# Fused attention and expert feed-forward block on Trainium2: a new tile order in the last group of heads and a rewritten last finish

## Chip, cores and metric

One core of a Trainium2 chip. The metric is the device time of one execution in microseconds; lower is better. A profile is one execution of its own, taken by the hardware profiler; its span runs from the first to the last instruction.

## The reference

A pre-norm transformer block on x of shape (1, 2048, 128) in float32: causal attention with 16 heads of 8 dimensions and rotary embedding, then a feed-forward part with a base layer, a shared low-rank expert and six low-rank experts of which the two with the largest gates count.

```python
def attn(x, w_qkv, w_out):                       # 16 heads, dh = 8
    q, k, v = split(x @ w_qkv)                   # to heads; rope on q and k
    scores = where(causal, q @ k.T * dh ** -0.5, finfo.min)
    return (softmax(scores) @ v).merge_heads() @ w_out

def ffn(x, base_W, base_b, shared_A, shared_B, routed_A, routed_B, router_W, router_b):
    base_out = x @ base_W.T + base_b
    shared_out = (x @ shared_A.T) @ shared_B.T                # rank 16
    logits = x @ router_W.T + router_b                        # 6 experts
    gate = softmax(logits)
    sparse_w = two largest gates of a row, others 0
    sparse_w = sparse_w / (sum(sparse_w) + 1e-6)
    routed = sum over e of sparse_w[e] * ((x @ routed_A[e].T) @ routed_B[e].T)
    return base_out + shared_out + routed

x = x + attn(layernorm(x), ...)
x = x + ffn(layernorm(x), ...)                   # layernorm without scale and shift, eps 1e-5
```

## The kernel before

The 2048 rows are 16 tiles of 128. `PREPS` are the stretches for which keys, queries and values are prepared, `PIECES` the query stretches that attention runs over, `FINISHES` those for which the output projection and the feed-forward part are done. The last piece and the last finish are tiles 14 and 15. Heads are worked in `NG` = 4 groups of four.

For one piece and group, `group_work` (line 85) lists the units: a unit is the scores of one key tile for the piece's query rows. In a piece of two query tiles a unit of kind "wide" is 128 keys by 256 query rows by four heads (1024 columns in PSUM), and the last key tile is a unit "half" with 128 query rows (512 columns). Only the last two units, key tiles t0 and t0 + 1, lie on the diagonal and are masked. Two units make a block; `plan` (line 94) numbers units and blocks, and `values` are issued a block at a time.

All engines walk the same list in their own program order, tied by semaphores:

- TensorE: `scores(u)` (line 926) into one of `NS` = 3 PSUM buffers, then `values(b)` (line 945) for blocks that are due, `LAG` = 5 units after their last unit, then `job(n)` (line 992) for other products.
- ScalarE: the exponential of unit u (line 588), straight from PSUM into one of `NPB` = 8 SBUF buffers `pbuf`; it signals `exp_ready`.
- GpSimd: masks (line 537) on diagonal units only, after their exponential; it signals `masked`. `values` of a block with a diagonal unit waits for `masked`.
- VectorE: `evacuate` (line 638) when a group's last block is done: transposes the sums in `po` and, in the last finish, divides them by the row sums (`normalise`, line 629). `take(n)` (line 731) does VectorE's part of the other jobs.
- SyncE: loads and stores.

A finish is the job list `FINISH` = A, O, M1, M2, M3, X, R, W1, W2, U, F. A: VectorE transposes the attention output into `feat`. O: output projection, added to the residual `xs` (line 779). M1, M2, M3: row moments (lines 614, 617), inverse root (lines 385, 386, 374 to 380), normalised rows `ln` (line 394). X: TensorE transposes `ln` (line 1018), VectorE copies it to `feat` (line 787). R: down projection with `wdown` (line 1021), whose 118 columns are 16 shared, 96 routed and 6 router columns; VectorE adds the router bias, subtracts the row maximum (lines 791 to 794) and copies the 112 low-rank columns to `low_rank` (line 796); ScalarE takes the exponential (line 599). W1 and W2: VectorE ranks the six gates by comparing each with each (lines 714 to 719) and scales the low-rank columns by the kept shares (lines 724 to 729, 803). U: TensorE transposes `low_rank` (line 1029), VectorE copies it to `lowT` (line 806). F: up projection onto the base products (lines 972, 1034), added to `xs` (line 809), which `store` (line 476) writes out. The constant 1 in column `RD` of `low_rank` brings in the bias of the base layer.

The earlier finishes are spread among the units (`PLACES`). The last one, `TAIL_JOBS`, runs alone after the loop. Each job of VectorE that feeds TensorE ends with a wait on its own last instruction (`then`) and a marker instruction (line 812) that signals `job_fed`. In the tail TensorE issues, before its product of each job, a number of matmuls that only keep it at work (`keep_warm`, line 1079):

```python
WARM = {"O": 8, "X": 16, "R": 3, "U": 16, "F": 3}
```

Of the kernel before, what the change touches and what calls it, by code (L numbers as in the profile page):

```python
# [80 lines left out]
FINISH_OF = [next(f for f, (t0, n) in enumerate(FINISHES) if t0 <= at < t0 + n) for at, _ in PIECES]  # L81
SWAPPED_PREPS = 3


def group_work(t0, tiles):

    if tiles == 4:
        return ([[("full", kt, (0,)), ("full", kt, (1,))] for kt in range(t0 + 1)]
                + [[("ends", t0 + 1, (0,)), ("ends", t0 + 1, (1,))], [("mid", t0 + 2, (0, 1))]])
    wide = [("wide", kt, (0, 1)) for kt in range(t0 + 1)] + [("half", t0 + 1, (0, 1))]  # L90
    return [wide[n:n + 2] for n in range(0, len(wide), 2)]


def plan():


    units, blocks = [], []
    for i, (t0, tiles) in enumerate(PIECES):
        for g in range(NG):
            work = group_work(t0, tiles)  # L100
            for n, members in enumerate(work):
                mine = list(range(len(units), len(units) + len(members)))
                for kind, kt, pairs in members:
                    units.append(dict(i=i, g=g, kind=kind, kt=kt, pairs=pairs, diagonal=kt >= t0, block=len(blocks)))
                blocks.append(dict(i=i, g=g, units=mine, first=n == 0, last=n == len(work) - 1,
                                   diagonal=any(units[u]["diagonal"] for u in mine)))
    return units, blocks
# [54 lines left out]
WARM = {"O": 8, "X": 16, "R": 3, "U": 16, "F": 3}  # L162
# [23 lines left out]
def schedule():  # L186


    jobs, at = [], {}
    for i, (mine, places) in enumerate(zip(ORDER, PLACES)):  # L190
        assert len(mine) == len(places)
        for job, place in zip(mine, places):
            at.setdefault(FIRST_UNIT[i] + place, []).append(len(jobs))
            jobs.append(job)
    tail = list(range(len(jobs), len(jobs) + len(FINISH)))
    jobs += [(name, NFINISH - 1) for name in FINISH]
    return jobs, at, tail


JOBS, JOBS_AT, TAIL_JOBS = schedule()  # L200
# [9 lines left out]
def build(nc, x, w_qkv, rope_c, rope_s, w_out, w_down, w_up, w_base, router_b, ident, head_sum,  # L210
# [3 lines left out]
    with ExitStack() as ctx:  # L214
# [59 lines left out]
        rank = sb("rank", [P, TC, E])  # L274

# [9 lines left out]

        def bank(n):

            return ps[:, 1, 0, :] if n == TAIL_JOBS[-1] else pm[:, :]
# [42 lines left out]
        y_ready = sem("y_ready")  # L331
        stored = sem("stored")
# [114 lines left out]
        def _(sp):  # L447
# [53 lines left out]
            for f in range(1, NFINISH):  # L501
                store(f)
            sp.wait_ge(stored, 16 * NFINISH)
# [38 lines left out]
        def _(act):  # L542
# [54 lines left out]
            nt = FINISHES[-1][1]  # L597
            act.wait_ge(logits_ready, NFINISH)
            nc.scalar.activation(gate[:, 0:nt, :], lg[:, 0:nt, :], ACT.Exp).then_inc(logits_exp, 1)  # L599

        @block.vector
        def _(dve):
# [128 lines left out]
            def take(n):  # L731
# [4 lines left out]
                product = bank(n)  # L736
# [74 lines left out]
                if n in FEEDS:  # L811
                    nc.vector.engine_nop().then_inc(job_fed, 1)  # L812

# [107 lines left out]
            for n in TAIL_JOBS:  # L921
                take(n)

        @block.tensor
        def _(pe):
# [66 lines left out]
            def job(n):  # L992
# [5 lines left out]
                product = bank(n)  # L998
# [20 lines left out]
                elif name == "R":  # L1019
# [3 lines left out]
                    if n in TAIL_JOBS:  # L1023
                        ins.then_inc(job_full, 1)
                        base(bank(TAIL_JOBS[-1]), nt)
                        return
# [3 lines left out]
                elif name == "F":  # L1030
                    if n not in TAIL_JOBS:
                        base(product, nt)
# [50 lines left out]

            pe.wait_ge(warm_ready, 1)
# [39 lines left out]
            for n in TAIL_JOBS:  # L1124
                keep_warm(WARM.get(JOBS[n][0], 0), kst[:, 0, 0:P], kst[:, 0, 0:CH])
                job(n)
# [56 lines left out]
```

## Time and profile before

| | us |
|---|---|
| median of 3 runs (lowest to highest) | 319.71 (319.04 to 320.12) |
| profiled execution, device time | 319.8 |
| its span | 318.1 |
| TensorE busy (matmuls) in the span | 285.8 (90%) |
| ScalarE | 269.6 (85%) |
| VectorE | 146.3 (46%) |
| GpSimd | 57.5 (18%) |
| mean granted TensorE clock | 0.973 of full |

The page gives each engine's busy time, and the same in 40 equal slices. The timeline shows instructions in order of time, merged where several of a line follow each other ("x4"); a bracket behind one says how long its engine had been idle and what released it. PEld is TensorE's weight load, which overlaps its matmuls, and DVE is VectorE, ACT ScalarE, POOL GpSimd, SP SyncE. A float32 product shows as two instructions. A merged row runs from the start of its first instruction to the end of its last. Ends of matmuls are modelled.

### The profile page before, as it was taken

What the parts mean: (1) busy time and instruction counts of PE and PEld (TensorE: products, weight loads), DVE (VectorE), ACT (ScalarE), POOL (GpSimd) and SP (SyncE); (2) the same over time, 40 slices, a digit from 0 to 9 for tenths busy, and PEclk for the clock granted to TensorE, in tenths of its full rate; (3) what the DMA queues carried; (4) which work ended last, traced back from release to release, by engine and by line L of the source; (5) the groups of instructions that cost most, each with busy time, mean ns of one, the idle gap of its engine ahead of it and who ended that gap; (6) DMA issues with size and microseconds to landing.
All of it is one profiled execution on the core that took longest, in us unless ns stands there. A gap on an engine that the chain in (4) does not pass through costs nothing.

```text
span 318.1 us, 7501 instructions
## 1 busy us (share of the span) xinstructions
PE 285.8 (90%) x3006; PEld 103.8 (33%) x3008; DVE 146.3 (46%) x425; ACT 269.6 (85%) x300; POOL 57.5 (18%) x129
## 2 busy tenths in 40 slices
PE   7948883989899989899999998999999999999896
PEld 2613241222223422123313313443533333433353
DVE  6775596468875376956241003651000514101064
ACT  8567584779999798999999999999999999999700
POOL 0485141031330300403003020101001010110100
PEclk9966998799999999999999999999999999999999
DMA  6333137000550000160000100000100000000000
GB/s 173 112 93 92 26 103 190 10 1 2 152 148 0 23 15 1 35 165 2 0 3 0 36 2 2 0 3 2 35 2 3 2 2 0 2 19 2 3 0 16
DMA packets 15400, 11.75 MB, mean 37 GB/s; under 512 B 2033, under 2 KB 14178, under 8 KB 15362
## 3 DMA queue, kind: packets, MB, share of 16 engines
q1 hardware_dynamic: 14866, 10.90, 12.6%
q8 instruction: 25, 0.41, 0.6%
q10 hardware_dynamic: 432, 0.20, 0.2%
q0 software_dynamic: 64, 0.13, 0.1%
q14 instruction: 13, 0.11, 0.1%
HBM read 3.88 MB, written 1.05 MB: 16 GB/s over the span
## 4 chain that ended last, share of the span: by engine, by line
PE 37%; ACT 22%; DVE 21%; issue 15%; DMA 2%; SPq 1%; DVEq 1%; POOL 0%; ACTq 0%; POOLq 0%
ACT pbuf L588 22%; PE po L962 17%; PE ps L940 9%; PE pm L978 3%; DVE rest L665 3%; DMA xs<-x_dram 2%; PE ps L1082 2%; DVE rot L672 2%; DVE absmax L696 1%; PE pm L1021 1%; PE pm L1015 1%; DVE oq L647 1%; DVE rot L659 1%; DVE rest L682 1%; PE pm L972 1%
## 5 line engine op out<-in xcount | busy, mean ns | idle before, releaser
L588 ACT ACTIVATE pbuf<-ps 128x1024 f32<-128x1024 f32 (+1 forms) x280 | 253.9, 1068 | 24.6 <-PE ps L940 24.2
L962 PE MATMUL po<-pbuf,va 128*9 128x256 f32 (+3 forms) x1792 | 146.7, 433 | 9.3 <-DVE oq L647 7.0
L940 PE MATMUL ps<-qst,kst 64*128 64x256 bf16 (+3 forms) x896 | 97.7, 303 | 8.1 <-ACT pbuf L588 3.4
L537 POOL TENSOR_SCALAR_AFFINE_SELECT pbuf<-pbuf 128x256 f32<-128x256 f32 (+1 forms) x104 | 48.9, 492 | 231.6 <-ACT pbuf L588 230.4
L940 PEld LDWEIGHTS ps<-qst,kst 64*128 64x128 bf16 x896 | 30.3, 95 | 104.0 <-ACT pbuf L588 77.2
L962 PEld LDWEIGHTS po<-pbuf,va 128*9 128x9 f32 x1792 | 35.6, 90 | 66.7 <-issue 42.8
L647 DVE STREAM_TRANSPOSE oq<-po 128x256 f32<-128x256 f32 (+1 forms) x24 | 12.9, 536 | 84.7 <-PE po L962 84.4
L665 DVE TENSOR_TENSOR rest<-pm,sinT 32x512 f32<-32x512 f32 x16 | 11.0, 687 | 0.3
L978 PE MATMUL pm<-xnT,wqkv 128*128 128x512 f32 x16 | 9.0, 644 | 1.9 <-DVEq L812 1.3
L1082 PE MATMUL ps<-kst 128*128 128x512 bf16 x44 | 10.5, 379 | 0.2 <-issue 0.2
L806 DVE COPY lowT<-pm 113x512 f32<-113x512 f32 (+1 forms) x5 | 2.9, 585 | 16.6 <-PE pm L1029 16.6
L614 DVE BATCH_NORM_STATS2 stats<-xs 128x6 f32<-128x128 f32 x32 | 7.1, 282 | 4.8 <-DMA xs<-x_dram 3.3
L599 ACT ACTIVATE gate<-lg 128x12 f32<-128x12 f32 x1 | 0.2, 213 | 10.4 <-DVE lg L794 10.4
L809 DVE TENSOR_TENSOR xs<-pm,xs 128x512 f32<-128x512 f32 (+1 forms) x4 | 2.5, 624 | 12.0 <-PE pm L1034 12.0
L779 DVE TENSOR_TENSOR xs<-pm,xs 128x512 f32<-128x512 f32 (+1 forms) x5 | 2.9, 585 | 9.2 <-PE pm L1015 9.2
L1082 PE MATMUL ps<-xnT 128*128 128x512 bf16 x16 | 5.2, 499 | 1.5 <-DVE xnT L868 1.5
L672 DVE TENSOR_TENSOR rot<-rot,rest 128x512 f32<-128x512 f32 (+1 forms) x10 | 6.1, 608 | 0.3
L1082 PEld LDWEIGHTS ps<-kst 128*128 128x128 bf16 x46 | 4.4, 97 | 4.5 <-issue 0.2
L545 ACT COPY kst<-fillers 128x2048 f32<-128x2048 f32 x3 | 5.7, 1897 | 0.0
L549 ACT COPY qst<-fillers 128x2048 f32<-128x2048 f32 x3 | 5.7, 1895 | 0.0
L682 DVE TENSOR_TENSOR rest<-rot,parts 128x512 f32<-128x512 f32 (+1 forms) x8 | 5.6, 694 | 0.3
L787 DVE COPY feat<-pm 128x512 f32<-128x512 f32 (+1 forms) x5 | 2.9, 585 | 5.6 <-PE pm L1018 5.6
(115 smaller groups left out, 184.6 us busy)
## 6 DMA issues: line engine op xcount, KB each, us to landing
qst<-parts SPq DMA_DIRECT2D x18, 128.0 KB, 2.4
kst<-parts SPq DMA_DIRECT2D x18, 128.0 KB, 2.5
xs<-x_dram SPq DMA_DIRECT2D x4, 256.0 KB, 4.1
cosT<-rope_c_dram SPq DMA_DIRECT2D x4, 256.0 KB, 4.4
sinT<-rope_s_dram SPq DMA_DIRECT2D x4, 256.0 KB, 5.6
out_dram<-xs SPq DMA_DIRECT2D x3, 256.0 KB, 2.3
kst<-parts SPq DMA_DIRECT2D x11, 64.0 KB, 2.1
qst<-parts SPq DMA_DIRECT2D x8, 64.0 KB, 2.0
```

What stands on the lines that cost most here:

```text
L537: ins = nc.gpsimd.affine_select(out=edge, in_=edge, compare_op=ALU.is_ge, fill=0.0, base=0, pattern=[[0, edge.shape[1]], [1, P]], channel_ ...
L545: nc.scalar.copy(kst[:, :, c * CH:(c + 1) * CH].bitcast(F32), fillers[:, 0:1].unsqueeze(2).broadcast_to([P, NP, CH // 2])).then_inc(filled, 1)
L588: nc.scalar.activation(probs[:, :, 0:width], ps[:, u % NS, :, 0:width], ACT.Exp, scale=SCALE).then_inc(exp_ready, 1)
L614: ins = nc.vector.bn_stats(stats[:, t, :], xs[:, tile + t, :])
L647: nc.vector.transpose(oq[:, g, mine, :].rearrange("p b r -> p (b r)"), po[:, 0:nt * P]).then_inc(o_free, 1)
L665: ins = nc.vector.tensor_tensor(rest[there:there + HALF, which, cols], product[here:here + HALF, :], sinT[here:here + HALF, c % 2, cols], ...
L672: return nc.vector.tensor_tensor(rot[:, which, cols], rot[:, which, cols], rest[:, which, cols], ALU.add)
L682: then(nc.vector.tensor_tensor(rest[:, which, cols], rot[:, which, cols], parts[:, which, 0, cols], ALU.subtract))
L940: ins = nc.tensor.matmul(ps[:, u % NS, e, place:place + n], side(kst, e)[:, g * 2 + pair, key:key + P], side(qst, e)[:, g * 2 + pair, q:q ...
L962: ins = nc.tensor.matmul(po[32 * j:32 * j + DH + 1, q0:q0 + n], va[:, kt, g * GH + j, :], pbuf[:, u % NPB, at:at + n], start=blk["first"] ...
L978: return nc.tensor.matmul(product, wqkv[:, which, :], xnT[:, chunk(p) % 2, local(p)], start=True, stop=True)
L1082: nc.tensor.matmul(ps[:, 1, 1, :], left, right, start=True, stop=True)
```

## The change

In the last group of heads of the last piece, the unit list is turned so that the two masked units come first, and the last block is split into two blocks of one unit. The tail jobs are replaced by one written-out sequence `end_of_chunk` on VectorE and TensorE, with semaphores of its own and no marker instructions:

- rows are only centred (mean subtracted) before they are transposed; the inverse root is computed after that. The scale of a row is applied to the logits, and to the final sum in the last instructions; the bias column gets the reciprocal of the scale (variance + eps, times the inverse root).
- ScalarE makes the copy of the transposed rows, and that of the 16 shared columns; the 96 routed columns are read by VectorE from PSUM as they are gated.
- experts are ranked by their logits, not by their exponentials. The comparison "greater" goes to a buffer of its own, `end_over`, and the difference to the maximum to `above`.
- the final sum is made tile by tile, and each tile has a store of its own.
- warm-up matmuls: 8, 7, 2, 14, 2 in place of 8, 16, 3, 16, 3.

```diff
+END, END_TILES = FINISHES[-1]
...
-def group_work(t0, tiles):
+def group_work(t0, tiles, last):
...
     wide = [("wide", kt, (0, 1)) for kt in range(t0 + 1)] + [("half", t0 + 1, (0, 1))]
+    if last:
+        wide = wide[-2:] + wide[:-2]
     return [wide[n:n + 2] for n in range(0, len(wide), 2)]
...
     for i, (t0, tiles) in enumerate(PIECES):
         for g in range(NG):
-            work = group_work(t0, tiles)
+            end = (i, g) == (NPIECE - 1, NG - 1)
+            work = group_work(t0, tiles, end)
+            if end:
+                work[-1:] = [[unit] for unit in work[-1]]
             for n, members in enumerate(work):
...
-WARM = {"O": 8, "X": 16, "R": 3, "U": 16, "F": 3}
+WARM_O, WARM_X, WARM_R, WARM_U, WARM_F = 8, 7, 2, 14, 2
...
-    tail = list(range(len(jobs), len(jobs) + len(FINISH)))
-    jobs += [(name, NFINISH - 1) for name in FINISH]
-    return jobs, at, tail
-JOBS, JOBS_AT, TAIL_JOBS = schedule()
...
-            for f in range(1, NFINISH):
+            for f in range(1, NFINISH - 1):
                 store(f)
-            sp.wait_ge(stored, 16 * NFINISH)
+            for t in range(END_TILES):
+                sp.wait_ge(y_ready, NFINISH + t)
+                sp.dma_start(out_t[:, END + t:END + t + 1, :], xs[:, END + t:END + t + 1, :]).then_inc(stored, 16)
+            sp.wait_ge(stored, 16 * (NFINISH - 1 + END_TILES))
...
-            nt = FINISHES[-1][1]
-            act.wait_ge(logits_ready, NFINISH)
-            nc.scalar.activation(gate[:, 0:nt, :], lg[:, 0:nt, :], ACT.Exp).then_inc(logits_exp, 1)
+            act.wait_ge(end_rows_turned, 1)
+            nc.scalar.copy(feat[:, 0:END_TILES * P], pm[:, 0:END_TILES * P]).then_inc(end_input, 1)
+            act.wait_ge(end_logits, 1)
+            nc.scalar.activation(gate[:, 0:END_TILES, :], above[:, 0:END_TILES, 0, :], ACT.Exp).then_inc(end_exp, 1)
+            by_tile = pm[:, 0:END_TILES * P].rearrange("p (t d) -> p t d", t=END_TILES)
+            nc.scalar.copy(low_rank[:, 0:END_TILES, 0:R], by_tile[:, :, 0:R]).then_inc(end_shared, 1)
...
+            def end_of_chunk():
+                f, nt = NFINISH - 1, END_TILES
+                tiles, wide = slice(END, END + nt), nt * P
+                by_tile = pm[:, 0:wide].rearrange("p (t d) -> p t d", t=nt)
+                last = ps[:, 1, 0, 0:wide].rearrange("p (t d) -> p t d", t=nt)
+                scale = rstd[:, 0, :]
+                nc.vector.transpose(feat[:, 0:wide],
+                                    att[:, f % 2, 0:wide // SQ, :, :].rearrange("p b g d -> p (b g d)")).then_inc(end_turned, 1)
+                dve.wait_ge(end_summed, 1)
+                then(nc.vector.tensor_tensor(xs[:, tiles, :], by_tile, xs[:, tiles, :], ALU.add))
+                spread(END, 0, nt)
+                for t in range(nt):
+                    nc.vector.tensor_scalar(ln[:, t, :], xs[:, END + t, :], mv[:, 0, t, 0:1], None,
+                                            ALU.subtract).then_inc(end_rows, 1)
+                inverse_sqrt(nc.vector, then, 0, nt)
+                then(nc.vector.tensor_tensor(low_rank[:, 0:nt, RD], var[:, 0, 0:nt], scale[:, 0:nt], ALU.mult))
+                dve.wait_ge(ffn_in, 16 * 5)
+                dve.wait_ge(end_down, 1)
+                mine, top, less = lg[:, 0:nt, :], chosen[:, 0:nt], above[:, 0:nt, 0, :]
+                for t in range(nt):
+                    ins = nc.vector.scalar_tensor_tensor(lg[:, t, :], by_tile[:, t, RD:RD + E], scale[:, t:t + 1],
+                                                         rbias[:, :], ALU.mult, ALU.add)
+                then(ins)
+                then(nc.vector.tensor_reduce(top, mine, AX.X, ALU.max))
+                nc.vector.tensor_tensor(less, mine, top.unsqueeze(2).broadcast_to([P, nt, E]),
+                                        ALU.subtract).then_inc(end_logits, 1)
+                shape = [P, nt, E, E]
+                this, other = mine.unsqueeze(3).broadcast_to(shape), mine.unsqueeze(2).broadcast_to(shape)
+                tied, over = ties[:, 0:nt], end_over[:, 0:nt]
+                then(nc.vector.tensor_tensor(tied, other, this, ALU.is_equal))
+                nc.vector.tensor_tensor(over, other, this, ALU.is_gt)
+                then(nc.vector.tensor_tensor(tied, tied, low[:, :, :].unsqueeze(1).broadcast_to(shape), ALU.mult))
+                then(nc.vector.tensor_tensor(over, over, tied, ALU.add))
+                then(nc.vector.tensor_reduce(rank[:, 0:nt, :], over, AX.X, ALU.add))
+                dve.wait_ge(end_exp, 1)
+                kept, total, share = rank[:, 0:nt, :], small[:, 0:nt], gate[:, 0:nt, :]
+                nc.vector.tensor_reduce(total, share, AX.X, ALU.add)
+                then(nc.vector.scalar_tensor_tensor(kept, kept, 1.5, share, ALU.is_lt, ALU.mult))
+                then(nc.vector.tensor_reduce(top, kept, AX.X, ALU.add))
+                then(nc.vector.scalar_tensor_tensor(total, total, 1e-6, top, ALU.mult, ALU.add))
+                then(nc.vector.reciprocal(total, total))
+                then(nc.vector.tensor_tensor(share, kept, total.unsqueeze(2).broadcast_to([P, nt, E]), ALU.mult))
+                dve.wait_ge(end_shared, 1)
+                nc.vector.tensor_tensor(low_rank[:, 0:nt, R:RD].rearrange("p t (e r) -> p t e r", e=E),
+                                        by_tile[:, :, R:RD].rearrange("p t (e r) -> p t e r", e=E),
+                                        gate[:, 0:nt, :].unsqueeze(3).broadcast_to([P, nt, E, R]),
+                                        ALU.mult).then_inc(end_routed, 1)
+                dve.wait_ge(end_low_turned, 1)
+                nc.vector.tensor_copy(lowT[0:RD + 1, 0:nt, :].rearrange("p t d -> p (t d)"),
+                                      pm[0:RD + 1, 0:wide]).then_inc(end_low, 1)
+                dve.wait_ge(end_full, 1)
+                for t in range(nt):
+                    nc.vector.scalar_tensor_tensor(xs[:, END + t, :], last[:, t, :], scale[:, t:t + 1], xs[:, END + t, :],
+                                                   ALU.mult, ALU.add).then_inc(y_ready, 1)
...
+            def end_of_chunk():
+                hot = kst[:, 0, 0:P], kst[:, 0, 0:CH]
+                tile = lambda t: slice(t * P, (t + 1) * P)
+                keep_warm(WARM_O, *hot)
+                pe.wait_ge(end_turned, 1)
+                for t in range(END_TILES):
+                    ins = nc.tensor.matmul(pm[:, tile(t)], feat[:, tile(t)], wout[:, :], start=True, stop=True)
+                ins.then_inc(end_summed, 1)
+                keep_warm(WARM_X, *hot)
+                for t in range(END_TILES):
+                    pe.wait_ge(end_rows, t + 1)
+                    ins = nc.tensor.transpose(pm[:, tile(t)], ln[:, t, :], idf[:, :])
+                ins.then_inc(end_rows_turned, 1)
+                keep_warm(WARM_R, *hot)
+                pe.wait_ge(end_input, 1)
+                for t in range(END_TILES):
+                    ins = nc.tensor.matmul(pm[:, t * P:t * P + RD + E], feat[:, tile(t)], wdown[:, :], start=True, stop=True)
+                ins.then_inc(end_down, 1)
+                base(ps[:, 1, 0, :], END_TILES)
+                keep_warm(WARM_U, *hot)
+                pe.wait_ge(end_shared, 1)
+                pe.wait_ge(end_routed, 1)
+                for t in range(END_TILES):
+                    ins = nc.tensor.transpose(pm[0:RD + 1, tile(t)], low_rank[:, t, 0:RD + 1], idf[:, :])
+                ins.then_inc(end_low_turned, 1)
+                keep_warm(WARM_F, *hot)
+                pe.wait_ge(end_low, 1)
+                for t in range(END_TILES):
+                    ins = nc.tensor.matmul(ps[:, 1, 0, tile(t)], lowT[0:RD + 1, t, :], wup[:, :], start=False, stop=True,
+                                           skip_group_check=True)
+                ins.then_inc(end_full, 1)
...
-            for n in TAIL_JOBS:
-                keep_warm(WARM.get(JOBS[n][0], 0), kst[:, 0, 0:P], kst[:, 0, 0:CH])
-                job(n)
+            end_of_chunk()
 
 
 def rope_tables(order):
```

## Rows read from the trace of the kernel before

**Rows 1.** Page, span and granted TensorE clock in 40 slices (tenths).

```profile
span 318.1 us, 7501 instructions
...
PEclk9966998799999999999999999999999999999999
```

**Rows 2.** Windows: stretch, its length, busy us per engine, granted clock, DMA share, GB/s.

```profile
53.00:56.00 3.00, 0.90 (x12) 0.42 (x16) 1.95 (x2) 0.00 (x0) 0.00 (x0) 0.50 0.80 223
284.00:300.00 16.00, 14.85 (x228) 5.43 (x228) 0.88 (x3) 16.00 (x19) 1.73 (x4) 1.00 0.01 3
```

**Rows 3.** Timeline, loop's end: start, us, engine, line, operation, count, idle before.

```profile
297.18 1.05 PE L962 MATMUL po<-pbuf,va 128*9 128x256 f32 x16
...
298.16 0.29 PE L940 MATMUL ps<-qst,kst 64*128 64x128 bf16 x4
...
298.38 1.91 PE L962 MATMUL po<-pbuf,va 128*9 128x256 f32 x32
299.62 1.35 POOL L537 TENSOR_SCALAR_AFFINE_SELECT pbuf<-pbuf 128x512 f32<-128x512 f32 x3 [12.89 <-ACT pbuf L588]
...
301.03 0.84 PE L962 MATMUL po<-pbuf,va 128*9 128x256 f32 x16 [0.73 <-POOL pbuf L537]
```

**Rows 4.** Line 588's last three exponentials: ns min/median/max, first and last start.

```profile
L588 ACT ACTIVATE pbuf<-ps x3: 853/1255/1269, 297.4 to 299.2; 128x1024 f32<-128x1024 f32 x2, 128x512 f32<-128x512 f32 x1
```

**Rows 5.** Timeline, first half of the last finish.

```profile
303.54 0.52 PEld L1015 LDWEIGHTS pm<-wout,feat 128*128 128x128 f32 x4 [0.34 <-DVEq L812]
...
305.55 0.17 DVE L385 TENSOR_SCALAR var<-mv 128x2 f32<-128x2 f32 x1
...
307.33 0.60 DVE L394 TENSOR_SCALAR ln<-xs,mv,rstd 128x128 f32<-128x128 f32 x2
...
308.05 0.44 PE L1018 MATMUL pm<-idf,ln 128*128 128x128 f32 x2 [0.34 <-DVEq L812]
...
309.06 0.70 PE L1021 MATMUL pm<-wdown,feat 128*128 128x118 f32 x4
```

**Rows 6.** Groups by line and shape, ScalarE: busy us, mean ns, idle before.

```profile
L545 ACT ACT_TABLE_LOAD x1 | 1.3, 1283 | 0.8 <-PEq L1177 0.8
...
L554 ACT COPY xnT<-pm 128x256 f32<-128x256 f32 x1 | 0.4, 373 | 0.2 <-PE pm L1090 0.2
```

**Rows 7.** Timeline, second half of the last finish, to the transposes.

```profile
309.80 0.17 DVE L791 TENSOR_TENSOR lg<-pm,rbias 128x12 f32<-128x12 f32 x1 [0.85 <-PE pm L1021]
309.94 3.23 PEld L1082 LDWEIGHTS ps<-kst 128*128 128x128 bf16 x16
...
310.20 0.17 DVE L794 TENSOR_TENSOR lg<-lg,small 128x12 f32<-128x12 f32 x1
310.29 0.38 DVE L796 COPY low_rank<-pm 128x224 f32<-128x224 f32 x1
...
310.72 0.23 DVE L714 TENSOR_TENSOR ties<-gate 128x72 f32<-128x72 f32 x1
...
313.13 0.36 DVE L803 TENSOR_TENSOR low_rank<-low_rank,gate 128x192 f32<-128x192 f32 x1
...
313.60 0.47 PE L1029 MATMUL pm<-idf,low_rank 128*113 128x128 f32 x2
```

**Rows 8.** Timeline, last sum and store.

```profile
315.39 0.42 DVE L809 TENSOR_TENSOR xs<-ps,xs 128x256 f32<-128x256 f32 x1 [0.86 <-PE ps L1034]
315.85 0.37 SPq L479 DMA_DIRECT2D out_dram<-xs  x1
```

**Rows 9.** DMA issues of the stores: count, KB each, us to landing.

```profile
out_dram<-xs SPq DMA_DIRECT2D x3, 256.0 KB, 2.3
...
out_dram<-xs SPq DMA_DIRECT2D x2, 128.0 KB, 1.8
```

**Rows 10.** Timeline of SyncE's queue: two issues in a row.

```profile
30.19 0.34 SPq L491 DMA_DIRECT2D wout<-w_out_dram  x1
30.58 0.43 SPq L491 DMA_DIRECT2D wdown<-w_down_dram  x1
```

More of the change, by code:

```diff
@@ L194, in schedule @@
             jobs.append(job)
-    tail = list(range(len(jobs), len(jobs) + len(FINISH)))
-    jobs += [(name, NFINISH - 1) for name in FINISH]
-    return jobs, at, tail
-JOBS, JOBS_AT, TAIL_JOBS = schedule()
+    return jobs, at
+JOBS, JOBS_AT = schedule()
 IS_PRODUCT = [name in PRODUCT_JOBS for name, _ in JOBS]
@@ L274, in build @@
         rank = sb("rank", [P, TC, E])
+        end_over = sb("end_over", [P, END_TILES, E, E])
         rmax = sb("rmax", [P, TC, H])
@@ L284, in build @@
         pm = ctx.enter_context(nc.psum_tensor("pm", [P, CH], F32))
-        def bank(n):
-            return ps[:, 1, 0, :] if n == TAIL_JOBS[-1] else pm[:, :]
         def first_bank(p, name):
@@ L331, in build @@
         y_ready = sem("y_ready")
+        end_turned = sem("end_turned")
+        end_summed = sem("end_summed")
+        end_rows = sem("end_rows")
+        end_rows_turned = sem("end_rows_turned")
+        end_input = sem("end_input")
+        end_down = sem("end_down")
+        end_logits = sem("end_logits")
+        end_exp = sem("end_exp")
+        end_shared = sem("end_shared")
+        end_routed = sem("end_routed")
+        end_low_turned = sem("end_low_turned")
+        end_low = sem("end_low")
+        end_full = sem("end_full")
         stored = sem("stored")
@@ L735, in take @@
                     dve.wait_ge(job_full, PRODUCTS[n])
-                product = bank(n)
+                product = pm[:, :]
                 if name in FINISH:
@@ L920, in _ @@
                         evacuate(b)
-            for n in TAIL_JOBS:
-                take(n)
+            end_of_chunk()
         @block.tensor
@@ L997, in job @@
                 pe.wait_ge(job_fed, FED[n])
-                product = bank(n)
+                product = pm[:, :]
                 tile = lambda t: slice(t * P, (t + 1) * P)
@@ L1022, in job @@
                                                start=True, stop=True)
[L1023 to L1026, printed above, removed]
                 elif name == "U":
@@ L1030, in job @@
                 elif name == "F":
-                    if n not in TAIL_JOBS:
-                        base(product, nt)
+                    base(product, nt)
                     for t in range(nt):
@@ L1123, in _ @@
                     values(b)
-            for n in TAIL_JOBS:
-                keep_warm(WARM.get(JOBS[n][0], 0), kst[:, 0, 0:P], kst[:, 0, 0:CH])
-                job(n)
+            end_of_chunk()
 def rope_tables(order):
```

## The prediction

> **What bounds the kernel now.** I read the page first: the span is 318.1 us and TensorE's granted clock is at its upper level (2.4 GHz) from the eleventh of the 40 slices to the end [rows 1]. The profiled run took 319.8 us, so 1.7 us lie around the span; the median of the three runs is 319.71, 0.1 below it. All sums below are made against the 319.8 run and then lowered by 0.1.
>
> Next the table of windows. From 284 to 300 us ScalarE is busy 16.00 of 16.00 us while TensorE has 14.85 [rows 2]: the loop over score tiles is bound by ScalarE's exponentials until the last one. Then the timeline of the loop's end. What the reader should see [rows 3]: the scores of the last unit at 298.16, then two whole blocks of value matmuls (32 matmuls, to 300.29), then GpSimd's masks of the last two tiles from 299.62 to about 301.0 (1.35 us busy in three instructions), and only then, at 301.03, the last 16 value matmuls, over at 301.87. The exponentials themselves [rows 4]: three start between 297.4 and 299.2, so 0.91 apart; the last full one starts at 298.3 and takes 1.269 us, so it ends at about 299.56 (it overlaps its neighbours in the record); the last one, half as wide, takes 0.853 and ends at 300.05. So a half tile holds ScalarE for 0.5 us and a full one for 0.91. The masks start 0.06 us after the 299.56 end: that is my price for a bare handoff between engines. Masks, not exponentials, release the last block: 0.98 us after the last exponential.
>
> After that one serial chain runs to the end, and VectorE carries most of it [rows 5, 7, 8]. TensorE fills its gaps with warm-up matmuls in program order, so two lines have to be compared in every gap.
>
> **Part 1: the masked tiles first, in the last group only.** The group has 15 full tiles and one half tile either way; ScalarE's work is the same and ends at about 300.06. The value matmuls after it no longer wait for masks, and the last block has one tile, not two. But TensorE takes its work in order. In the new order every exponential from the second on ends 0.91 - 0.50 = 0.41 earlier than the one in the same position now, except the last. TensorE follows ScalarE there, so its block of 297.18 and the scores at 298.16 [rows 3] move to about 296.77 and 297.75. The last scores are those of a full tile, some 0.1 us longer than the 0.22 until 298.38, so the remaining blocks start at 298.07. They are 16 + 16 + 8 + 8 matmuls. Two blocks in a row take 1.91 us, one alone at full width 1.05, so a block adds 0.86: 298.07 + 3 x 0.86 + 0.19 = 300.84. The last exponential is done at 300.06, in time for the last 8 matmuls at about 300.22. New end 300.84 against 301.87: gain 1.03. Best case, bound by ScalarE alone: 300.06 + 0.06 + 0.43 + 0.19 = 300.74, gain 1.13. Worst case: the two half tiles, now one unit apart, let ScalarE run dry. Between two releases of a score buffer lie two exponentials, 0.91 + 0.50 = 1.41 us, for a block of values (0.86) and a scores unit (up to 0.4), so there is just room; the same combination now passes once between groups without idle ScalarE [rows 2]. I allow 0 to 0.25 us of loss and take nothing.
> The masks of the new first block stand in GpSimd's queue behind the three instructions of the group before. Their values are due after the seventh scores of the group, some 4 us after their exponentials, and 2 x 1.35 us of masks [rows 3] fit in that: nothing. That cover would be gone if GpSimd had other work; it has none there.
>
> **Part 2: from the attention output to the logits.** VectorE's transposes, reciprocal and product right after the last block stay. The output projection is released by a VectorE marker instruction now (0.34 idle until 303.54 [rows 5]); the marker goes, which could give 0.05, but the eight warm-ups in front of it stay and end at about the same time: I take 0 of 0 to 0.05.
> Then the order changes. Now: moments done at 305.52, nine small instructions of the inverse root from 305.55 to 307.33 (1.78), two row normalisations of 0.60, marker, transposes at 308.05, VectorE's copy, down projection at 309.06, logits at 309.80 [rows 5, 7]. From 305.55 that is 4.25 us.
> New, from the same point A: two centrings, 0.60 (the same two rows of 128 elements, one operation less on each). They release the transposes; VectorE goes on with the nine instructions (1.78) and one more small one (0.20), so it is ready for the logits at A + 0.60 + 0.02 + 1.78 + 0.20 + 0.02 = A + 2.62. The other line: transposes start at A + 0.66, take 0.3 to 0.44, ScalarE's copy of 128x256 takes 0.37 [rows 6], its handoffs 0.06 to 0.12 each, the down projection 0.74 from 309.06 to 309.80: A + 2.2 to 2.4. VectorE is last, and the projection is hidden behind the inverse root. Gain 4.25 - 2.62 = 1.63. If ScalarE's or TensorE's handoffs are slower than in the rows, up to 0.3 of it goes. The two copies put on ScalarE stand behind an idle queue after 300.06. The trace has one table load in all, at the start, and copies and exponentials alternate later without another [rows 6]: no switching cost.
>
> **Part 3: routing.** Now, from the logits to the transposes: 309.80 to 313.60, 3.80 us [rows 7]. A small waited instruction costs 0.20 (1.78 / 9), one that nothing waits for 0.09 (310.20 to 310.29), the 72-element ones 0.23 and about 0.26 waited. New: two logit instructions in place of one, 0.28; maximum 0.20; difference 0.09; comparison "equal" 0.26; "greater", now unwaited, 0.15; product, sum, count 0.26 + 0.27 + 0.26; total, unwaited, 0.09; kept, sum, combination, reciprocal, share 5 x 0.20; gating 0.36; handoff 0.06, and 0.05 for the added waits: 3.33. The large removed term is the copy of 128x224 out of PSUM, which stood on VectorE from 310.29 until the comparison at 310.72: 0.43, now ScalarE's (at most the 0.37 of [rows 6], from an exponential that no longer holds the comparisons up). Gain 0.47, between 0.3 and 0.55. TensorE's line there: down projection done by A + 2.4, base products, then 14 warm-ups at 3.23 / 15 = 0.215 [rows 7], 3.0 us, the first at most 0.14 after the logits' release: that ends at A + 5.5, while VectorE ends at A + 5.9. It stays covered; with 16 it would be about even.
>
> **Part 4: after the gating.** The copy of the turned low-rank features loses its marker: gain 0.05. At the end one sum of 0.42 and one store [rows 8] become two scaled sums of 128 columns and two stores. By the pair in [rows 5], 0.60 for both and, an estimate, 0.34 for the first. The first store is issued at +0.38; the second can follow 0.39 later (30.19 to 30.58, [rows 10]), at +0.77, against +0.46 now, so 0.31 later. It moves half the bytes. The stores of 256 KB land after 2.3 us, that of 128 KB after 1.8 [rows 9], so 64 KB less should give back 0.25; that leaves -0.06. If landing stays at 1.8, it is -0.31. I take -0.10, range -0.4 to 0. The Trainium skill (DMA: Bandwidth & Descriptors, Anatomy of one DMA) speaks against this part: a DMA's fixed cost of some 2 us doesn't depend on size, and bytes add only bytes / 436 GB/s. By that, halving 128 KB gives back an estimated 0.15 us, and this part would be -0.16. The fixed part agrees in kind with the trace's 1.8 us for a small store.
>
> **Sum.** 1.03 + 0 + 1.63 + 0.47 + 0.05 - 0.10 = 3.08 us. 319.8 - 3.08 - 0.1 = 316.6 us. Sum of the worst ends: 0.78 + 1.33 + 0.30 - 0.40 = 2.0, so 317.7; of the best: 1.13 + 0.05 + 1.63 + 0.55 + 0.05 = 3.4, so 316.3.
>
> **Rivals.** (a) TensorE's line takes VectorE's place in the finish: warm-ups, base products and handoffs are late in both long gaps by 0.3 to 0.4 each. For it: the margins are only 0.2 and 0.4 us. Against it: both are computed from rows at the same clock. Time 317.3.
> (b) Part 1 gives only 0.2: ScalarE runs dry near the two half tiles, or the three value blocks, in program order, are still what ends last. For it: 48 value matmuls stand behind the last scores in both versions, and TensorE has 1.15 us of slack in 16. Against it: the 0.73 us that TensorE idled for the masks is really gone. Time 317.4.
> (c) Slower: TensorE's clock falls to 1.2 GHz in the finish, since there are 33 warm-ups there instead of 46. The trace shows the lower level between 53 and 56 us (granted 0.50 [rows 2]), where TensorE was at work for 0.90 of 3 us. At it a warm-up takes 0.43 (twice 0.215): the 8, 7 and 14 would then outlast VectorE by about 1.7 + 1.1 + 2.9, and the matmul groups would add some 2: 7.7 us, time 324.3. It decides once the clock falls before about 307. Against it: the longest idle stretch of TensorE after the change is shorter than the 0.73 us before 301.03, which leaves the clock at its upper level now. The Trainium skill (TensorE: Matmul & The Clock Gate, What's actually happening) says the gate follows how busy the engine has been recently; by it the denser end would keep the clock.
> (d) (a) and (b) together, with a late second store: 318.0 to 318.9, too near to be told from no change when over 318.75.
>
> **Chances.** About 0.3% (0.96 us) is what a measurement of this kernel can tell from no change. Forecast, 316.6 within 0.6: 0.60. (a) 0.16, (b) 0.10, (d) 0.06, more gain than the best sum (below 316.0): 0.05, (c) 0.03. Faster 0.92, same 0.05, slower 0.03. The range takes in the forecast, (a) and (b): 315.9 to 317.9.
>
> **What would show it.** Right: the last value block over at 300.8 with no idle TensorE before it; logits 2.6 us after the moments with VectorE, not TensorE, released last; 3.3 us from logits to the transposes; last store issued 0.8 us after the last product. Wrong: gaps in ScalarE between 285 and 290, a clock below 1.0 after 300, VectorE idle before the logits or before the gating, a table load, or a second store that lands over 2 us after its issue.

## The result and the profile after

| | before | after |
|---|---|---|
| median, us (lowest to highest) | 319.71 (318.76 to 320.30) | 316.36 (315.97 to 316.77) |
| ratio, 95% interval | | 0.990 (0.9876 to 0.9925) |
| profiled execution, us | 319.8 | 316.77 |
| its span, us | 318.1 | 315.0 |

The changed kernel is 3.35 us faster by the medians and 3.0 by the profiled runs. The page after the change, to be read beside [rows 1]: span, and granted TensorE clock in tenths for each of 40 slices.

```profile
span 315.0 us, 7475 instructions
...
PEclk9976998699999999999999999999999999999999
```

The clock is at its upper level to the end, as before.

Executions differ in when they come to the end of the loop: what lies ahead of it is the same code, but the first mark below stands at 283.49 to 284.50 in the fourteen profiled executions. So I compare distances between marks that every version has, not clock times. The first mark is the start of the half tile's scores in the group before the last (283.92 before, 284.14 after); the others follow in the table. The one for the moments is the start of the second moment instruction (aggregation). The page rounds spans to a tenth; I use the trace's hundredths: 318.06 before, 315.03 after.

Where several profiled executions have the same code in a stretch, these distances agree within 0.02 us; so a difference of 0.1 us between two of them is read below as one of the code.

| stretch, us | before | after | gain | predicted |
|---|---|---|---|---|
| half tile's scores to the end of the last value block | 17.95 | 16.92 | 1.03 | 1.03 |
| to the moments (aggregation starts) | 3.40 | 3.34 | 0.06 | 0 |
| to the logits | 4.53 | 2.65 | 1.88 | 1.63 |
| to the second transposes | 3.80 | 3.47 | 0.33 | 0.47 |
| to the last product | 1.05 | 0.96 | 0.09 | 0.05 |
| to the end of the span | 3.41 | 3.55 | -0.14 | -0.10 |
| sum | 34.14 | 30.89 | 3.25 | 3.08 |

The rows behind it. Timeline of the changed kernel at the loop's end (start, us, engine, line, operation, count, idle before), to be read beside [rows 3]:

```profile
285.60 2.76 POOL L554 TENSOR_SCALAR_AFFINE_SELECT pbuf<-pbuf 128x512 f32<-128x512 f32 x6 [12.93 <-ACT pbuf L605]
...
296.97 1.05 PE L1037 MATMUL po<-pbuf,va 128*9 128x256 f32 x16
...
297.95 0.39 PE L1015 MATMUL ps<-qst,kst 64*128 64x256 bf16 x4
...
298.28 2.78 PE L1037 MATMUL po<-pbuf,va 128*9 128x256 f32 x48
300.31 0.24 PEld L1037 LDWEIGHTS po<-pbuf,va 128*9 128x9 f32 x8 [0.19 <-ACT pbuf L605]
```

The six masks from 285.60 are the three of the group before, which stood there already, and the three of the last group, which have moved here; TensorE waits for none of them. The last scores start at 297.95, and from 298.28 one unbroken run of 48 value matmuls ends at 301.06; where 0.73 us of idle TensorE stood in [rows 3] there is none. The only wait in it is the weight load of the last block for the last exponential, 0.19 us, which hides under the matmuls still running. ScalarE doesn't run dry near the two half tiles. Window of the changed kernel, to be read beside [rows 2]:

```profile
284.00:300.00 16.00, 14.78 (x232) 5.63 (x232) 0.88 (x3) 16.00 (x19) 2.70 (x6) 1.00 0.01 3
```

Timeline of the changed kernel from the output projection to the logits, beside [rows 5]:

```profile
302.67 0.52 PEld L1161 LDWEIGHTS pm<-wout,feat 128*128 128x128 f32 x4 [0.28 <-DVE feat L841]
...
304.69 0.48 DVE L847 TENSOR_SCALAR ln<-xs,mv 128x128 f32<-128x128 f32 x2
...
305.03 0.52 PE L1166 MATMUL pm<-idf,ln 128*128 128x128 f32 x2
305.08 0.16 DVE L399 TENSOR_SCALAR var<-mv 128x2 f32<-128x2 f32 x1
...
305.59 0.37 ACT L615 COPY feat<-pm 128x256 f32<-128x256 f32 x1 [5.33 <-PE pm L1166]
...
306.02 0.70 PE L1171 MATMUL pm<-wdown,feat 128*128 128x118 f32 x4
...
306.86 0.16 DVE L850 TENSOR_TENSOR low_rank<-var,rstd 128x2 f32<-128x2 f32 x1
...
307.05 0.35 DVE L855 SCALAR_TENSOR_TENSOR lg<-pm,rstd,rbias 128x6 f32<-128x6 f32 x2
307.44 0.17 DVE L858 TENSOR_REDUCE chosen<-lg 128x2 f32<-128x12 f32 x1
```

The order has turned round: rows are centred from 304.69, transposed from 305.03, ScalarE's copy runs from 305.59 to 305.96 and the down projection from 306.02 to 306.72; beside them, on VectorE, the inverse root runs from 305.08. VectorE is done at 307.02 and takes the logits at 307.05 with no wait. Note that the root starts 0.39 after the first centring, and that the two logit instructions take 0.39 until the maximum at 307.44.

Timeline of the changed kernel in the routing part, beside [rows 7]:

```profile
307.85 0.21 ACT L617 ACTIVATE gate<-above 128x12 f32<-128x12 f32 x1 [1.89 <-DVE above L859]
307.97 0.17 ACT L619 COPY low_rank<-pm 128x32 f32<-128x32 f32 x1
308.00 0.23 DVE L865 TENSOR_TENSOR end_over<-lg 128x72 f32<-128x72 f32 x1
...
310.01 0.36 DVE L878 TENSOR_TENSOR low_rank<-pm,gate 128x192 f32<-128x192 f32 x1
...
310.52 0.45 PE L1178 MATMUL pm<-idf,low_rank 128*113 128x128 f32 x2 [0.32 <-DVE low_rank L878]
```

ScalarE's exponential and its copy of the shared columns are over at 308.14, while VectorE compares. They are not waited for. The gating ends at 310.37 and the transposes start 0.15 later, after 0.32 us in which TensorE had no work left: VectorE is last here too.

Timeline of the last sums and stores, and then the issues of stores with KB each and us to landing, beside [rows 8, 9]:

```profile
312.23 0.61 DVE L887 SCALAR_TENSOR_TENSOR xs<-ps,rstd,xs 128x128 f32<-128x128 f32 x2 [0.81 <-PE ps L1183]
312.61 0.82 SPq L519 DMA_DIRECT2D out_dram<-xs  x2
```

```profile
out_dram<-xs SPq DMA_DIRECT2D x3, 256.0 KB, 2.3
...
out_dram<-xs SPq DMA_DIRECT2D x1, 128.0 KB, 1.9
out_dram<-xs SPq DMA_DIRECT2D x2, 64.0 KB, 1.6
```

### The profile page after: what moved, and what is told of

Same layout as the page of the kernel before. It is cut to its first block, busy times and chain, and to the rows that moved or that the text cites. A ratio compares the mean times of both kernels' runs of the same rounds, so it can differ in the third digit from the quotient of the medians.

```text
span 315.0 us, 7475 instructions
## 1 busy us (share of the span) xinstructions
PE 284.0 (90%) x2995; PEld 103.0 (33%) x2995; DVE 146.0 (46%) x426; ACT 270.1 (86%) x302; POOL 57.5 (18%) x129
## 3 DMA queue, kind: packets, MB, share of 16 engines
HBM read 3.88 MB, written 1.05 MB: 16 GB/s over the span
## 4 chain that ended last, share of the span: by engine, by line
PE 39%; DVE 23%; ACT 20%; issue 14%; DMA 2%; DVEq 1%; SPq 1%; ACTq 0%
ACT pbuf L605 19%; PE po L1037 19%; PE ps L1015 10%; PE pm L1053 3%; DVE rest L685 3%; DMA xs<-x_dram 2%; DVE rot L692 2%; DVE absmax L716 1%; DVE oq L667 1%; DVE rot L679 1%; DVE rest L702 1%; PE pm L1090 1%; PE pm L1096 1%; PE pm L1047 1%; DVE parts L709 1%
## 5 line engine op out<-in xcount | busy, mean ns | idle before, releaser
L1152 PE MATMUL ps<-kst 128*128 128x512 bf16 x33 | 8.0, 379 | 0.0
L679 DVE TENSOR_TENSOR rot<-pm,cosT 128x512 f32<-128x512 f32 x4 | 2.8, 692 | 5.6 <-PE pm L1053 5.1
L711 DVE TENSOR_TENSOR parts<-rest,parts 128x512 bf16<-128x512 f32 (+1 forms) x8 | 5.2, 645 | 0.3
L716 DVE TENSOR_REDUCE absmax<-rot 128x2 f32<-128x1024 f32 (+1 forms) x5 | 5.0, 996 | 0.0
```

What stands on the lines that cost most here:

```text
L716: then(nc.vector.tensor_reduce(absmax[:, :], rot[:, :, local(p)], AX.X, ALU.max, apply_absolute_value=True))
L1152: nc.tensor.matmul(ps[:, 1, 1, :], left, right, start=True, stop=True)
```

## Experiments

All have the computation of the reference except where it is said. The two parts alone and the better version at the end were timed several times; the others rest on one profiled execution each, and are read by the distances between marks, not by their total time. Clock times of these rows are those of their own execution.

**The two parts, each alone.** First the kernel before with the new order and the split only:

```diff
+    if last:
+        wide = wide[-2:] + wide[:-2]
...
+            if end:
+                work[-1:] = [[unit] for unit in work[-1]]
```

> Part 1 alone on the kernel before: masked units first in the last group, last block in two. Measured from the scores of the half tile of the group before to the end of the last value block: before 17.95 us. Theory (the wait for the masks was the cost, TensorE's program order is what is left): 16.92, no idle TensorE before the last block, total 1.0 us under before (318.7). Rival (b) (ScalarE runs dry at the two half tiles or the queue of value blocks ends at the same time anyway): 17.75, total 319.5.

Measured: 318.69 us median against 319.81, ratio 0.9968 (0.9948 to 0.9988). Timeline of this kernel, first and last mark of the loop's end:

```profile
283.69 0.29 PE L945 MATMUL ps<-qst,kst 64*128 64x128 bf16 x4
...
297.82 2.78 PE L967 MATMUL po<-pbuf,va 128*9 128x256 f32 x48
```

297.82 + 2.78 - 283.69 = 16.91 us, against 17.95. The wait for the masks is gone, and 48 matmuls in program order are what is left. Rival (b), with a gain of only 0.2 us, falls.

Then the changed kernel without these lines, so the new finish behind the old order:

> The new finish alone, with the old order of units and blocks. Theory (the two parts don't overlap): the loop ends as before (17.95), and the finish is 2.2 to 2.3 us shorter, total 317.4. Rival (a part of the finish's gain came from TensorE's line being earlier after part 1): under 1.8 us.

Measured: 317.65 us median, ratio 0.9929 (0.9904 to 0.9954); loop's end 17.94. Timeline, last value block of this kernel:

```profile
301.07 0.84 PE L1033 MATMUL po<-pbuf,va 128*9 128x256 f32 x16 [0.73 <-POOL pbuf L550]
```

The wait for the mask is back as it was. From the moments to the logits 2.65, to the second transposes 3.47, to the last product 0.96: the same as with both parts. Gains by the medians: 1.1 + 2.2 us, against 3.35 for both. The parts add up.

**The split of the last block.** The changed kernel without its second edit to the blocks:

```diff
-            if end:
-                work[-1:] = [[unit] for unit in work[-1]]
```

> The changed kernel with the last block of two units as one block. Theory: its 16 matmuls wait for the last exponential and then take 1.05 instead of 0.75, so the loop's end is 0.30 later than after the change (17.2 instead of 16.9 by the measure above). Rival (program order alone decides, the split is for nothing): no later.

Timeline of this kernel, the two marks:

```profile
284.42 0.28 PE L1013 MATMUL ps<-qst,kst 64*128 64x128 bf16 x4
...
298.55 3.09 PE L1035 MATMUL po<-pbuf,va 128*9 128x256 f32 x48
```

298.55 + 3.09 - 284.42 = 17.22 us against 16.92: the split is worth 0.30 of the 1.03 and the order alone 0.73. Whole block or not, the number of matmuls is the same; but the whole one holds the first tile's matmuls back until the last exponential.

**Warm-ups.** The changed kernel with the old numbers:

```diff
-WARM_O, WARM_X, WARM_R, WARM_U, WARM_F = 8, 7, 2, 14, 2
+WARM_O, WARM_X, WARM_R, WARM_U, WARM_F = 8, 16, 3, 16, 3
```

> The changed kernel with the old numbers of warm-ups (8, 16, 3, 16, 3). Theory (two lines in every gap; VectorE's is last by only 0.2 to 0.3 us now): the transposes of the centred rows start 1.5 later, the logits 1.35 later, and the gap before the second transposes gives 0.15 more, 1.5 us in all. Rival (VectorE's chain sets the end and warm-ups are free): under 0.2.

Timeline of this kernel: warm-ups, transposes, logits.

```profile
303.47 3.62 PE L1152 MATMUL ps<-kst 128*128 128x512 bf16 x16
...
306.92 0.38 PE L1166 MATMUL pm<-idf,ln 128*128 128x128 f32 x2
...
308.62 0.35 DVE L855 SCALAR_TENSOR_TENSOR lg<-pm,rstd,rbias 128x6 f32<-128x6 f32 x2 [1.35 <-PE pm L1171]
```

The sixteen warm-ups hold the transposes until 306.92, though the rows were ready at about 305.3, and the logits now wait 1.35 us for TensorE. From the moments to the logits 3.97 instead of 2.65 (+1.32), to the second transposes 3.59 instead of 3.47 (+0.12). Together that is 1.44, near the 1.5 expected; 0.06 comes back before the last product, so the old numbers would have taken 1.38 of the gain of 3.25. The rival, under 0.2, falls.

The changed kernel with none:

```diff
-WARM_O, WARM_X, WARM_R, WARM_U, WARM_F = 8, 7, 2, 14, 2
+WARM_O, WARM_X, WARM_R, WARM_U, WARM_F = 0, 0, 0, 0, 0
```

> The changed kernel with no warm-up in the finish. Theory (the clock falls when TensorE has little to do): the granted clock goes to 0.5 within the finish, the later matmul groups get longer, and the total is 0.5 to 1.5 us more. Rival (the finish is too short for a fall, VectorE sets the end): clock stays 1.0, total the same or up to 0.1 less.

Windows of this kernel (stretch, length, busy us of TensorE, weight load, VectorE, ScalarE, GpSimd, then granted clock, DMA share, GB/s), and then its matmul groups:

```profile
300.00:303.00 3.00, 1.38 (x20) 0.74 (x12) 1.32 (x4) 0.03 (x1) 0.00 (x0) 1.00 0.00 0
303.00:306.00 3.00, 0.90 (x5) 0.40 (x3) 2.53 (x13) 0.37 (x1) 0.00 (x0) 0.84 0.00 0
306.00:308.00 2.00, 1.99 (x8) 1.69 (x8) 1.31 (x9) 0.00 (x0) 0.00 (x0) 0.50 0.00 0
```

```profile
302.44 0.71 PE L1161 MATMUL pm<-wout,feat 128*128 128x128 f32 x4 [1.62 <-DVE feat L841]
...
304.79 0.65 PE L1166 MATMUL pm<-idf,ln 128*128 128x128 f32 x2 [1.64 <-DVE ln L847]
...
305.91 1.21 PE L1171 MATMUL pm<-wdown,feat 128*128 128x118 f32 x4 [0.46 <-ACT feat L615]
...
311.99 1.22 PE L1183 MATMUL ps<-wup,lowT 113*128 113x128 f32 x4 [0.52 <-DVE lowT L883]
```

TensorE was idle for 1.62 us before 302.44 and for 1.64 before 304.79; the granted clock, 1.00 up to 305, was 0.50 from 305.5 to the end (finer windows of the same execution). The down projection takes 1.21 us instead of 0.70, the last product 1.22 instead of 0.71. From the first mark to the end it is 32.13 us instead of 30.89: 1.24 more, although no warm-up is in anybody's way: 0.45 of it before the logits, 0.30 between the second transposes and the last product, 0.50 behind the start of that product. The two runs together: a warm-up costs nothing only while it ends ahead of the other line, and leaving all out costs 1.2. Numbers between 0 and 33 were not tried.

**What the copy on ScalarE is worth.** The changed kernel with that copy on VectorE, behind the centring:

```diff
-            nc.scalar.copy(feat[:, 0:END_TILES * P], pm[:, 0:END_TILES * P]).then_inc(end_input, 1)
...
+                dve.wait_ge(end_rows_turned, 1)
+                nc.vector.tensor_copy(feat[:, 0:wide], pm[:, 0:wide]).then_inc(end_input, 1)
                 inverse_sqrt(nc.vector, then, 0, nt)
```

> The changed kernel with the copy of the turned rows on VectorE again, between the centring and the inverse root. Theory (the root hides the transposes and the projection only because the copy is ScalarE's): the root starts 0.9 later, logits 0.9 to 0.95 later. Rival (half of the gain would be there with any engine, since VectorE can wait): 0.45 or less.

Timeline of this kernel: copy, first instruction of the root, logits.

```profile
304.94 0.43 DVE L848 COPY feat<-pm 128x256 f32<-128x256 f32 x1 [0.42 <-PE pm L1166]
305.28 0.16 DVE L399 TENSOR_SCALAR var<-mv 128x2 f32<-128x2 f32 x1
...
307.24 0.35 DVE L855 SCALAR_TENSOR_TENSOR lg<-pm,rstd,rbias 128x6 f32<-128x6 f32 x2
```

VectorE idles 0.42 us for the transposes and copies for 0.43; from the moments to the logits it is 3.49 instead of 2.65, so 0.84 more. That is a little under the 0.9 expected and well over the rival's 0.45. Nearly half of the 1.88 depends on a second engine being free.

**How far TensorE's line is behind.** The changed kernel with only the first two instructions of the root (its scale is then a rough estimate, so the last two tiles are not computed to the reference's precision):

```diff
-                inverse_sqrt(nc.vector, then, 0, nt)
+                then(nc.vector.tensor_scalar(v, mv[:, 0, 0:nt, 1], EPS, None, ALU.add))
+                then(nc.vector.tensor_scalar(r.bitcast(I32), v.bitcast(I32), -0.5, float(0x5F3759DF), ALU.mult, ALU.add))
```

> The changed kernel with seven of the nine instructions of the last inverse root left out (only the first estimate is kept, so rows 14 and 15's tiles are scaled inexactly; the other work is the same). VectorE's line to the logits is 7 x 0.197 = 1.38 us shorter. Theory (TensorE's and ScalarE's line is 0.29 us behind it): the logits start only 0.25 to 0.3 us sooner, released by the down projection. Rival (VectorE alone sets the time to the logits): 1.38 sooner.

Timeline of this kernel: the bias column's instruction, then the logits.

```profile
305.34 0.16 DVE L852 TENSOR_TENSOR low_rank<-var,rstd 128x2 f32<-128x2 f32 x1
...
306.72 0.35 DVE L857 SCALAR_TENSOR_TENSOR lg<-pm,rstd,rbias 128x6 f32<-128x6 f32 x2 [1.22 <-PE pm L1173]
```

VectorE was ready at 305.50 and waited 1.22 us for the down projection. From the moments to the logits it is 2.46 instead of 2.65: 1.38 us less work gives 0.19 us. The line through ScalarE and TensorE is done only 0.19 us before VectorE's, less than the 0.25 to 0.3 that I expected.

**Ranking by exponentials again, in the changed kernel.**

```diff
-                this, other = mine.unsqueeze(3).broadcast_to(shape), mine.unsqueeze(2).broadcast_to(shape)
+                by = gate[:, 0:nt, :]
+                this, other = by.unsqueeze(3).broadcast_to(shape), by.unsqueeze(2).broadcast_to(shape)
+                dve.wait_ge(end_exp, 1)
```

> The changed kernel with experts ranked by their exponentials again. Theory: the comparisons wait for ScalarE's exponential, 0.35 us more. Rival (the gain in routing is all from the copy that left VectorE): under 0.1.

Timeline of this kernel, the first comparison:

```profile
308.13 0.23 DVE L866 TENSOR_TENSOR ties<-gate 128x72 f32<-128x72 f32 x1 [0.28 <-ACT gate L617]
```

From the logits to the transposes 3.84 instead of 3.47: 0.37 more. This is more than the whole gain of the routing part, 0.33: with the copy on ScalarE but the old ranking the stretch is 3.84, no better than the 3.80 before, since VectorE now idles 0.28 us for the exponential that the copy covered. The other half, ranking by logits with the copy still on VectorE, was not run.

**Stores.** One store of 128 KB behind both sums:

```diff
-            for t in range(END_TILES):
-                sp.wait_ge(y_ready, NFINISH + t)
-                sp.dma_start(out_t[:, END + t:END + t + 1, :], xs[:, END + t:END + t + 1, :]).then_inc(stored, 16)
+            sp.wait_ge(y_ready, NFINISH - 1 + END_TILES)
+            sp.dma_start(out_t[:, END:END + END_TILES, :], xs[:, END:END + END_TILES, :]).then_inc(stored, 16)
```

> The changed kernel with one store of 128 KB after both sums. Theory (issue of the second store 0.14 later, landing 0.2 to 0.25 sooner): the end is 0.05 to 0.1 later than with two stores. Rival (fixed cost of a store whatever its size): 0.1 to 0.14 sooner.

Timeline of this kernel, the sums and the store:

```profile
312.14 0.61 DVE L886 SCALAR_TENSOR_TENSOR xs<-ps,rstd,xs 128x128 f32<-128x128 f32 x2 [0.81 <-PE ps L1182]
312.77 0.37 SPq L518 DMA_DIRECT2D out_dram<-xs  x1
```

From the last product to the end 3.59 us (314.98 - 311.39) instead of 3.55: two stores are only 0.04 better than one behind the same two sums. That is little, but the seven other executions with these two stores have 3.53 or 3.54 there. The one store is issued 0.16 sooner and takes 0.2 longer to land. The rival with a cost whatever the size falls, narrowly: 64 KB land after 1.6 us, 128 KB after 1.8 or 1.9, 256 KB after 2.3.

The second store from ScalarE's queue. In what was expected of it, "those edits" are the two of the next version.

```diff
-            for t in range(END_TILES):
-                sp.wait_ge(y_ready, NFINISH + t)
-                sp.dma_start(out_t[:, END + t:END + t + 1, :], xs[:, END + t:END + t + 1, :]).then_inc(stored, 16)
+            sp.wait_ge(y_ready, NFINISH)
+            sp.dma_start(out_t[:, END:END + 1, :], xs[:, END:END + 1, :]).then_inc(stored, 16)
...
+            act.wait_ge(y_ready, NFINISH + 1)
+            nc.scalar.dma_start(out_t[:, END + 1:END + 2, :], xs[:, END + 1:END + 2, :]).then_inc(stored, 16)
```

> Only the second of those edits: the second store from ScalarE's queue. Theory: from the first instruction of the last product to the end 0.14 us less than after the change (3.52 there). Rival: no less.

Timeline of this kernel, last product and stores:

```profile
311.84 0.71 PE L1184 MATMUL ps<-wup,lowT 113*128 113x128 f32 x4
...
312.96 0.34 SPq L518 DMA_DIRECT2D out_dram<-xs  x1
313.23 0.38 ACTq L620 DMA_DIRECT2D out_dram<-xs  x1
```

From the last product to the end it is 3.37 us (315.21 - 311.84) instead of 3.55 (the expectation had 3.52 for it; the executions have 3.53 to 3.55): at least the 0.14 expected.

**A version with both leftovers taken.** The store's edit, and the bias column no longer waited for; then the changed kernel once more beside it:

```diff
-                then(nc.vector.tensor_tensor(low_rank[:, 0:nt, RD], var[:, 0, 0:nt], scale[:, 0:nt], ALU.mult))
+                nc.vector.tensor_tensor(low_rank[:, 0:nt, RD], var[:, 0, 0:nt], scale[:, 0:nt], ALU.mult)
```

> The changed kernel with two edits: the bias column's instruction is no longer waited for before the logits (0.20 to 0.09, so 0.11 sooner), and the second store is issued from ScalarE's queue as soon as its sum is done (0.14 sooner). Theory: the issue of the second store stands at 0.04 after its sum and the span is 0.25 us shorter. Rival (a store's issue on ScalarE's queue takes longer than on SyncE's, or the two stores meet in the same rings): the second edit gives nothing or costs 0.1, the span is 0 to 0.1 shorter.

> The changed kernel once more, beside the next one on the same chip: 3.0 to 3.4 us under before, ratio 0.990.

Timeline of the better version: bias column, logits, last sums, both stores.

```profile
306.31 0.17 DVE L851 TENSOR_TENSOR low_rank<-var,rstd 128x2 f32<-128x2 f32 x1
...
306.40 0.35 DVE L856 SCALAR_TENSOR_TENSOR lg<-pm,rstd,rbias 128x6 f32<-128x6 f32 x2
...
311.57 0.61 DVE L888 SCALAR_TENSOR_TENSOR xs<-ps,rstd,xs 128x128 f32<-128x128 f32 x2 [0.81 <-PE ps L1184]
311.95 0.34 SPq L518 DMA_DIRECT2D out_dram<-xs  x1
312.22 0.38 ACTq L620 DMA_DIRECT2D out_dram<-xs  x1
```

The logits start 0.09 behind the bias column instead of 0.19, and the last product to the end takes 3.38. From the first mark to the end: 30.61 us, against 30.87 for the changed kernel on the same chip: 0.26 less, as expected (0.11 before the logits, 0.15 at the stores). The medians, 315.88 and 316.02 against 319.96 (ratios 0.9890, 0.9853 to 0.9927, and 0.9886, 0.9855 to 0.9917), can't tell the two apart. So the total time doesn't show that this version is faster; only the stretches that were changed do, in one profiled execution of each.

## Why the prediction was right, point by point

- **What bounds the loop's end.** The predicted 300.84 for the end of the values, from the marks of before, is 283.92 + 16.92 = 300.84 measured. The steps on the way hold too: on the clock of before the last scores start at 297.73 (predicted 297.75) and the value matmuls at 298.06 (298.07). The step that carried it was to walk TensorE's queue and not to stop at "the last exponential plus one block". Rival (b) had a chance of 0.10; the run with the order alone refutes it.
- **To the logits.** Mechanism right, two sizes off. The centring pair was put at 0.62 from the row of the old pair; without the second operation each takes 0.28, they start 0.20 apart, and the root doesn't wait for the second: 0.39. That is 0.23 of the 0.25 by which the term was too small. The cover held, but it is thinner than the sum had it: the other line is done 0.19 ahead of VectorE's, not 0.2 to 0.4. The range of this term, 1.33 to 1.63, allowed only for loss, and the measured 1.88 lies outside it.
- **Rival (a)**, TensorE's line in the place of VectorE's, was near: 0.19 us away before the logits and 0.32 before the second transposes. With the old warm-up numbers it comes true (+1.32 and +0.12 us), and so it shows what the smaller numbers are for.
- **Routing.** 0.33 and not 0.47. The mis-sized term is the pair of logit instructions, 0.39 and not 0.28: I took the price of an unwaited instruction without a per-row scale (0.09); with it, and 6 elements from PSUM, it is 0.22 long and about 0.13 to the next. The other 0.04 is the handoff to the transposes, 0.15 and not 0.11. And I gave the gain to the copy alone; the run with the old ranking shows that this is not enough, since all of the gain goes with the ranking by logits. What that ranking gives without the copy is open.
- **Markers.** 0.06 ahead of the output projection, where I took 0 of 0 to 0.05: the warm-ups were no bound there, since the projection's first weight load already waited for the marker, 0.34 us before the change [rows 5]. 0.09 in place of 0.05 between transposes and product. No run has the markers alone.
- **Stores.** -0.14 against -0.10, inside the range. The second issue came 0.41 behind the first (0.82 for the two), and the smaller store landed 0.2 sooner, not 0.25. The Trainium skill (DMA: Bandwidth & Descriptors, Anatomy of one DMA) gives its fixed 2 us and its slope for DMAs that GpSimd issues in software, which the prediction didn't say. The term by them, an estimated -0.16, was as near, but the times themselves don't agree: on SyncE's queue here 64 KB have landed after 1.6 us, less than the page's fixed part alone, and from 128 KB to 256 KB it takes 0.4 to 0.5 us more, where the page's slope gives an estimated 0.3. On ScalarE's queue, with no issue ahead of it, the stretch is 3.37 against 3.41 before, so the term would have been +0.04.
- **Rival (c)**, a fall of the clock, exists, but 33 warm-ups were enough against it: the clock stays at its upper level with them and falls without any. Its price of 7.7 us assumed warm-ups at the lower level and was not tested; without them the fall costs 1.2.
- **The total.** Part of its nearness is luck. The terms were off by +0.25, +0.06 and +0.04 on one side and by -0.14 and -0.04 on the other, so that the sum is off by only 0.17.

## What to carry to other kernels

Where a serial chain on one engine meets a chain through others, move what only scales a row behind the products: the scale is then computed beside them, and the gain is at most the shorter of the two lines, so write both down. Filler work that keeps an engine's clock up is part of its line: each time the cover gets shorter, count it again. And a wait for masks at the end of a loop can go away with the order of its tiles alone (0.73 us here, with the same work on every engine); cutting the last block down to the last tile gave 0.30 more.

## What the runs showed of the hardware that I had not expected

With no filler, TensorE's clock had fallen to its lower level, 1.2 GHz (granted 0.50 from 305.5 us), after two idle stretches of only 1.6 us with 0.7 us of matmuls between them; groups of four float32 products then took 1.21 us instead of 0.70. And a VectorE instruction on 6 elements from PSUM with a per-row scale took 0.22 us, more than the 0.17 of one on 12 elements from PSUM without it [rows 7].
